# One ScalarE block of four Gelus in place of two blocks of two in the first matmul of a dense expert layer

## What is computed

```python
xn = _layernorm(x, axis=-1)
# attention: k = xn @ Wk, v = xn @ Wv, rotors and phases (sin, cos),
# four cumulative sums over time, gates, then @ Wo
router_probs = softmax(x_flat @ gate_w); expert_idx = argmax(router_probs)
out = zeros
for e in range(8):
    h = gelu(x_flat @ w1[e] + b1[e], approximate=False)   # 1024 -> 4096
    y = h @ w2[e] + b2[e]                                 # 4096 -> 1024
    out = out + where(expert_idx == e, expert_w, 0)[:, None] * y
return x + attention + out
```

## Time and profile before

| what | value |
|---|---|
| median of 2 runs | 5876.63 us (5840.19 and 5913.08) |
| profiled execution, time | 5848.73 us |
| its span on the slowest core (core 5) | 5847.2 us |
| spans of the 8 cores | 5773.9 to 5847.2 us |
| mean granted TensorE clock, core 5 | 0.920 |
| instructions on core 5 | 52387 |

### The profile page before, as it was taken

How to read it: one execution, slowest core, us unless ns; L and a number is a source line. 1 busy time by engine, 2 the same in 40 slices (tenths; PEclk the granted TensorE clock), 3 DMA queues, 4 the chain that set the end, 5 groups by cost and what they waited for, 6 DMA issues and landing times.

```text
span 5847.2 us, 52387 instructions; the slowest of 8 cores (5773.9 to 5847.2 us)
## 1 busy us (share of the span) xinstructions
PE 4170.2 (71%) x18224; PEld 1839.4 (31%) x18224; DVE 1429.8 (24%) x2651; ACT 2075.9 (36%) x2496; POOL 432.0 (7%) x727
## 2 busy tenths in 40 slices
PE   1122587787787678787887778877788778877782
PEld 0022233333333233333333333333333333333331
DVE  2233122212221222122213331122311333023231
ACT  0011343434343444343434333344323433234440
POOL 1000000000000000000010000010000100010000
PEclk9999998899898889898998899998999999988996
DMA  5876664445346545455454646565545654553333
GB/s 77 125 117 102 163 154 127 130 131 152 115 141 165 139 124 151 126 156 122 134 161 135 151 145 166 154 163 141 150 124 149 163 139 142 157 156 133 130 114 120
DMA packets 371633, 810.04 MB, mean 139 GB/s; under 512 B 71080, under 2 KB 246440, under 8 KB 337584
## 3 DMA queue, kind: packets, MB, share of 16 engines
q0 software_dynamic: 226624, 409.01, 32.0%
q1 hardware_dynamic: 144752, 397.69, 20.6%
HBM read 930.36 MB, written 157.29 MB: 186 GB/s over the span
## 4 chain that ended last, share of the span: by engine, by line
PE 51%; ACT 20%; DMA 12%; DVE 10%; issue 6%; DVEq 1%; SPq 0%; ACTq 0%; POOLq 0%
PE f_y L959 26%; PE f_h L909 18%; ACT L112 9%; DMA w1ring<-w1c 5%; ACT f_h L112 4%; DMA w2c<-w 3%; DMA ln_x<-xfh 2%; PE a_kv L628 2%; PE a_kv L623 2%; DVE accf L112 2%; DVE ln_stg L112 1%; ACT a_bnt L112 1%; ACT a_bnp L112 1%; DMA o_x<-xown 1%; PE ln_tr L404 1%
## 5 line engine op out<-in xcount | busy, mean ns | idle before, releaser
L909 PE MATMUL f_h<-f_xn,w1ring 128*128 128x512 bf16 x8192 | 1985.6, 399 | 953.1 <-ACT f_h L112 838.5
L112 ACT ACT_TABLE_LOAD x688 | 882.7, 1283 | 3464.2 <-PE f_h L909 1962.0
L959 PE MATMUL f_y<-f_w,f_h 128*128 128x512 bf16 x8192 | 1787.4, 380 | 71.4 <-DVE accf L112 51.9
L909 PEld LDWEIGHTS f_h<-f_xn,w1ring 128*128 128x128 bf16 x8192 | 803.8, 101 | 2121.5 <-issue 1334.4
L959 PEld LDWEIGHTS f_y<-f_w,f_h 128*128 128x128 bf16 x8192 | 801.8, 98 | 1050.8 <-issue 95.5
L112 ACT ACTIVATE f_h<-f_h,b_s 128x512 bf16<-128x512 f32 x1024 | 703.7, 687 | 74.3 <-PE f_h L909 23.0
L112 DVE SCALAR_TENSOR_TENSOR accf<-f_y,se_tm,accf 128x512 bf16<-128x512 f32 x224 | 168.2, 751 | 1329.7 <-PE f_y L959 1309.1
L836 POOL DMA_DIRECT2D f_w<-w2c x512 | 273.3, 585 | 2780.1 <-PE f_y L959 2724.8
L112 DVE TENSOR_SCALAR a_tA<-a_bnp 128x512 f32<-128x512 f32 x64 | 27.7, 433 | 1660.0 <-ACT a_bnt L112 1660.0
L112 DVE TENSOR_TENSOR_SCAN a_cb<-a_p,carries,consts 128x512 f32<-128x512 f32 x256 | 328.6, 1284 | 27.6 <-DVE a_p L112 1.4
L404 PE MATMUL ln_tr<-ident_s,ln_xn 128*128 128x128 f32 x256 | 62.1, 424 | 359.7 <-DVE ln_xn L112 359.7
(11 more groups left out here) (69 smaller groups left out, 1427.8 us busy)
## 6 DMA issues: line engine op xcount, KB each, us to landing
w1ring<-w1c SPq DMA_DIRECT2D x256, 1024.0 KB, 6.8
f_w<-w2c POOLq DMA_DIRECT2D x512, 512.0 KB, 6.0
w1c<-w POOLq DMA_DIRECT2D x64, 1024.0 KB, 11.9
w2c<-w POOLq DMA_DIRECT2D x128, 512.0 KB, 7.0
f_xn<-xnscr SPq DMA_DIRECT2D x32, 1024.0 KB, 8.4
a_wk<-wkc SPq DMA_DIRECT2D x64, 256.0 KB, 6.5
a_wv<-wvc SPq DMA_DIRECT2D x64, 256.0 KB, 6.8
ln_x<-xfh SPq DMA_DIRECT2D x16, 512.0 KB, 5.9
```

The source lines that it names most:

```text
L112: ins = fn(*a, **k)
L909: ins = t.matmul(hps[ctg % NHPS][:, 0:FCH], w1ring[:, slot * KT * W1CO + kt * W1CO + ct * P: slot * KT * W1CO + kt * W1CO + (ct + 1) * P], ...
L959: ins = t.matmul(yps[tt][:, 0:MMW], hsb[:, kc * FCH + tt * P: kc * FCH + (tt + 1) * P], w2ring[:, slot * KCG * MMW + k2 * MMW: slot * KCG ...
```

## The change

The two ScalarE functions of a block (two Gelus each) become one function of four Gelus, emitted after the block's first pair of matmuls. Since the matmuls of the third and fourth `ct` are not yet emitted at that point, their semaphore values are computed (`base + ct - NHPS + 1`); they are the same values as before. The matmuls keep their two functions per block, and every wait of TensorE stays as it was.

```diff
-                    for ctb in range(0, NW1C, NHPS):
+                    def emit_f1_mms(ctb, e=e, c=c, cob=cob, slot=slot, sl=sl,
+                                    gcob0=gcob0):
                         @block.tensor
...
                                 tok_t_f1ct[(e, c, ctg)] = T.inc(ins)
 
+                    def emit_f1_gelus(e=e, c=c, cob=cob, gi=gi):
+                        base = T.n
+
                         @block.scalar
-                        def _(s, e=e, c=c, cob=cob, ctb=ctb, gi=gi):
+                        def _(s):
...
                             if pgi >= 0:
-                                grp = (cob * NW1C + ctb) // KCG
-                                ws.need(s, tok_t_hsbfree[(pgi, grp)])
-                            for ct in range(ctb, min(ctb + NHPS, NW1C)):
+                                for grp in sorted({(cob * NW1C + ct) // KCG
+                                                   for ct in range(NW1C)}):
+                                    ws.need(s, tok_t_hsbfree[(pgi, grp)])
+                            for ct in range(NW1C):
                                 ctg = cob * NW1C + ct
-                                ws.need(s, tok_t_f1ct[(e, c, ctg)])
+                                if (e, c, ctg) in tok_t_f1ct:
+                                    ws.need(s, tok_t_f1ct[(e, c, ctg)])
+                                else:
+                                    ws.need(s, (T, base + ct - NHPS + 1))
                                 ins = s.activation(
...
-                    tok_t_f1[(e, c, cob)] = tok_t_f1ct[(e, c,
-                                                        cob * NW1C + NW1C - 1)]
+
+                    emit_f1_mms(0)
+                    emit_f1_gelus()
+                    for ctb in range(NHPS, NW1C, NHPS):
+                        emit_f1_mms(ctb)
+                    tok_t_f1[(e, c, cob)] = (T, T.n)
                     au_tick()
```

More of the change, by code:

```diff
@@ L889, in _ @@
                                     [[KT * W1CO, P], [1, KT * W1CO]])))
-                    for ctb in range(0, NW1C, NHPS):
+                    def emit_f1_mms(ctb, e=e, c=c, cob=cob, slot=slot, sl=sl,
+                                    gcob0=gcob0):
                         @block.tensor
-                        def _(t, e=e, c=c, cob=cob, slot=slot, sl=sl, ctb=ctb,
-                              gcob0=gcob0):
+                        def _(t, ctb=ctb):
                             wt.need(t, tok_g_w1[gcob0 + cob])
```

## The result

The changed kernel takes 5808.73 us in the median of 16 runs, the kernel before 5854.99 us in the median of 15. Both medians include executions in which four of the eight cores, or all, had a lower granted clock, with either kernel (up to 6291 us); without them the ratio is 0.9909, with a 95% interval from 0.9886 to 0.9931. So the change gains 0.9%, about 53 us of 5855 (40 to 67). The forecast was 0.988, 68 us: right sign, right mechanism, slightly too large.

What follows compares the result with a forecast made beforehand. TensorE was taken to set the end, pausing for Gelus whose table load lies behind the wait. 5848.7 - 90 + 18 + 4 = 5781 us, ratio 0.988, range 5712 to 5848; chance of the forecast's mechanism 0.76.

Steps and rivals of the forecast that it cites:

- The count of loads: On ScalarE, one table load per function: 688 before, 432 after, 328 us less of ScalarE's time.
- Step (1): At a block's first pair of matmuls, 130 short TensorE waits on Gelus go, 0.69 us each: 90 us gained.
- Step (2): The 196 short waits at a block's second pair and the 49 long ones behind attention units stay.
- Step (3): One wait for `hsb` per block and one ScalarE branch less: both taken as 0, bounds 0 and 26 us of gain.
- Step (4): Shorter blocks make `w1ring` loads late: 18 us of the 90 given back on core 5, bounds 0 and 90.
- Step (5): Longer waits for late loads let one or two more stretches of matmuls run at 1.2 GHz: 4 us lost, bounds 0 and 14.
- 19 us at the most: Each of the 28 existing waits on `w1ring` loses about one boundary's gain, 28 x 0.69.
- The larger time below 5732: Chance of the kernel being faster by over 2%: 0.12 from the larger-gain rival, 0.02 from the forecast's low tail.
- All short waits going without being asked: ScalarE loads before waiting for TensorE, so short waits at both pairs go: 5643 us; one way of the larger gain, 0.12.
- The clock giving back 82 us: Fewer pauses keep TensorE at 2.4 GHz more, halving the slow matmuls' cost: 5695 us; another way of the larger gain, 0.12.
- The blocks becoming bound by `w1ring`: Weight loads set the pace, TensorE waits for DMA instead of Gelus: 5849 us; one way of nothing at all, 0.08.
- Nothing, or slower: Two rivals: no gain, 5849 us, chance 0.08; late loads with the clock falling behind them, about 5966 us, chance 0.04.

Runs made afterwards that it cites:

- load-ahead kernel: Kernel before, with a one-column Gelu on a scratch tile heading each of its 512 Gelu functions, ahead of the wait for TensorE: ratio 0.9732 to the kernel before.
- empty functions: Changed kernel plus one ScalarE function per block that does nothing, ahead of the four Gelus: ratio 0.9892 to the kernel before.
- kernels with three slots: Kernel before and changed kernel, each with three slots in `w1ring` in place of two: ratios 0.9898 and 0.9686 to the kernel before.
- changed kernel with three slots: Changed kernel with three slots in `w1ring` in place of two: ratio 0.9686 to the kernel before, profiled execution 5685.4 us.
- last kernel: Kernel before with three `w1ring` slots, one-column Gelus heading the Gelu functions and one-column Sins heading each attention unit's two functions: ratio 0.9358 to the kernel before.
- load ahead and three slots: Kernel before with a one-column Gelu heading each Gelu function and three slots in `w1ring`: ratio 0.9542 to the kernel before, profiled execution 5595.9 us.

## Why the prediction was right, point by point

**The count of loads** (one per ScalarE function, 688 to 432) and the place of the removed one: right, shown by the page after and by the load-ahead kernel. The Trainium skill (ScalarE activation tables: per-element evaluation and per-set limits, "Table sets in the compiler and the runtime") says that the compiler places the loads per block of the program. The traces agree, with 688, 432, 1200 and 264 loads for as many functions with activations.

**Step (1), 130 x 0.69 = 90 us.** Right. Eight cores lose 134 waits in the mean, 92 us (94 counted by starts); pairs stand at 4.15 and 3.45 us in turn.

**Step (2), what stays.** Right: 250 waits on core 5, for which the forecast had 245, and 250 on core 7, among them 49 long ones on each core. In us the long ones moved by 5 at the most on cores 0 and 3, but fell by 13 and 20 on cores 5 and 7; why is open.

**Step (3), the wait and the branch at 0.** Nothing speaks against it: the empty functions add no wait on Gelus, and step (1) comes out without a term for a branch. The single wait for `hsb` per block was not tested by itself.

**Step (4), 18 us given back at late loads.** This is the term that was too small, though not on the core for which it was made. I had carried the gains through with every load's duration as in the one trace. On core 5 the waits inside the loop grew from 104 to 117 us, 13 against 18. (The list of waits has 139 us in 36 waits there, against 130 and 35 forecast; 12 us of its growth are at the very first load, 27.8 us in place of 15.5, where the loop has not begun.) On cores 0, 6 and 7 the reckoning left 85 us or more of the gain, so hardly anything was to go back there, but the waits grew by 26, 44 and 71 us, and by 27 in the mean of eight. The loads did not keep the durations of the trace before: on core 7 the longest took 25.3 us in place of 15.8. And core 7, with the longest waits for `w1` of all, was the slowest and set the time. The "19 us at the most" for the waits that were there already did not hold as a bound for all: 22 waits per core became 32. I had also left out the other stream: waits for `w2` pieces grew by 5 to 15 us on the four cores, 7 in the mean of eight. That late loads do take gain back is what the kernels with three slots show, where `w1ring` takes back 6 us in the mean and the change is worth 104 us; they also show that the rest of the difference has other parts.

**Step (5), the clock, 4 us.** Between -4 and +23 us on the four cores, where my bounds were 0 and 14, and 6 in the mean of eight: the size was a guess, and that the mean comes near it is luck. Beside it, on cores 5 and 7 some 400 matmuls stood a little above the usual distance of 0.216 us and cost 17 us. What that is stays open; cores 4 and 6 have it too (13 and 15 us), while it is absent on cores 0 to 3 of the same execution and in the changed kernel with three slots, and there again, with 8 or 9 us, in the kernels with the load ahead.

**The sum.** The mean of the spans fell by 49 us and the forecast was 68. Steps (1) and (2) gave a little more than forecast, 101 us in place of 90; what was missed is 9 us at `w1ring`, 7 at `w2` pieces, 8 of spacing, 2 of slow matmuls and some 5 elsewhere. So part of the nearness is luck: 11 us more than forecast came in, against some 31 that were missed.

**The rivals.** All short waits going without being asked: excluded, 200 stayed. The clock giving back 82 us: excluded, 401 ns in the mean against 399. The blocks becoming bound by `w1ring`: my sign for it was 180 us of waits there, and the largest is 142. Nothing, or slower: outside the interval. The larger time below 5732 that I gave a chance of 0.14 is real, but it takes other edits than this change.

## What to carry to other kernels

Where each function of the source becomes a block of the program, count ACT_TABLE_LOAD against the functions; and look in the list by time at what stands on either side of a load. A load behind a wait for the producer adds its whole length to the chain over that buffer (1.28 us, of which 0.69 showed as a pause here); a one-column activation of the same function ahead of the wait moves it into idle time, here for 0.2 us. And before shortening a loop, ask what lands just in time for it, on every core and not on the slowest alone: with a third slot in the weight ring this change was worth twice as much.

## What the runs showed that I had not expected

A pair of 16 matmuls takes 4.15 us with one load per two Gelus and also with one per Gelu. 512 more loads cost 0.6%, since TensorE was bound by the chain over one load, and ScalarE's throughput of about 2.07 us per Gelu with its load comes to the same.

The Identity activations of the attention's first function ran behind a load made for Sin without one of their own (2886.03 to 2887.48 in the last kernel).

The waits for `w2` pieces grew with every gain: 19.5 us on the slowest core before, 35 with the change and three slots, 52 with the load ahead and three slots, and 62 in the last kernel. Among TensorE's waits in the expert loop they are now next, behind the 562 us that it waits mostly for the attention's activations.
